# A residual taken from normalised tiles: VectorE's add of the spikes uses a ratio per token, and GpSimd normalises x once less

## What is computed

```python
x = x + layernorm(attn(layernorm(x)))      # attn: time mix and channel mix, each ended by spikes
x = x + layernorm(ffn(layernorm(x)))       # ffn: ternary weights, swiglu, two hidden layers with gelu

def attn(x):                               # x here is already normalised once
    x = x + lif(time_mix(layer_norm(x, ln1_s, ln1_b), ...))
    x = x + lif(channel_mix(layer_norm(x, ln2_s, ln2_b), ...))
    return x
```

## Time and profile before

| | us |
|---|---|
| median of 3 runs (lowest to highest) | 785.07 (781.07 to 785.68) |
| profiled execution | 779.8 |
| its span | 777.8 |
| mean granted TensorE clock, share of full speed | 0.952 |
| TensorE busy | 620.4 (80%) |
| VectorE busy | 640.6 (82%) |
| ScalarE busy | 522.6 (67%) |
| GpSimd busy | 478.2 (61%) |

### The profile page before, as it was taken

The page is one execution under the profiler, slowest core; times in us unless marked ns, Lnnn a source line. Parts: engine busy times, 40 slices in busy tenths (PEclk is TensorE's granted clock), DMA queues, the critical chain, the costliest instruction groups (busy, mean ns, idle before and its releaser), DMA issues. The chain is left out here.

```text
span 777.8 us, 10326 instructions
## 1 busy us (share of the span) xinstructions
PE 620.4 (80%) x2241; PEld 368.2 (47%) x2241; DVE 640.6 (82%) x1585; ACT 522.6 (67%) x791; POOL 478.2 (61%) x592
## 2 busy tenths in 40 slices
PE   3165399888888979898888979898888979888884
PEld 1022146464545546464555546463545546455553
DVE  5889688998989898989889898989889898965541
ACT  2543376868687776858586776868587777857563
POOL 4333526767685857747585857757575858563533
PEclk9577589999999999999999999999999999999998
DMA  5020000000000000000000000000000000000000
GB/s 206 0 68 0 29 1 1 28 15 28 14 29 15 27 13 0 27 13 27 13 27 13 27 13 0 27 13 27 13 27 13 13 16 13 15 2 0 15 14 13
DMA packets 26384, 16.69 MB, mean 21 GB/s; under 512 B 1136, under 2 KB 25712, under 8 KB 26096
## 3 DMA queue, kind: packets, MB, share of 16 engines
q1 hardware_dynamic: 26352, 16.34, 6.9%
HBM read 12.14 MB, written 4.19 MB: 21 GB/s over the span
## 5 line engine op out<-in xcount | busy, mean ns | idle before, releaser
L1511 PE MATMUL p_f<-ac_lo,w_hi 128*128 128x512 f32 x320 | 145.7, 455 | 16.9 <-DVE ac_lo L291 9.1
L723 ACT ACTIVATE hid<-p_f,scale 128x512 f32<-128x512 f32 x128 | 87.9, 687 | 89.3 <-PE p_f L1511 89.3
L407 POOL TENSOR_TENSOR var<-mv,eps_row 128x4 f32<-128x4 f32 x64 | 34.3, 536 | 177.1 <-DVE mv L959 177.1
L1511 PE MATMUL p_f<-ac_hi,w_hi 128*128 128x512 f32 x320 | 129.5, 405 | 0.0
L1511 PE MATMUL p_f<-b_lo,w_hi 128*128 128x512 f32 x256 | 109.0, 426 | 2.8 <-DVE b_lo L291 1.2
L1511 PE MATMUL p_f<-b_hi,w_hi 128*128 128x512 f32 x256 | 101.1, 395 | 0.0
L718 ACT ACTIVATE ac_hi<-hid 128x512 fp32r<-128x512 f32 x128 | 80.8, 632 | 22.3 <-DVE hid L1160 20.2
L291 DVE TENSOR_TENSOR ac_lo<-hid,ac_hi 128x512 fp32r<-128x512 f32 x80 | 78.0, 987 | 20.9 <-ACT ac_hi L718 20.1
L1511 PEld LDWEIGHTS p_f<-ac_lo,w_hi 128*128 128x128 f32 x320 | 62.5, 195 | 53.8 <-issue 17.9
L420 POOL TENSOR_TENSOR rstd<-var,minus_half 128x4 f32<-128x4 f32 x64 | 82.4, 1288 | 2.5
L291 POOL TENSOR_TENSOR ac_lo<-hid,ac_hi 128x512 fp32r<-128x512 f32 x48 | 66.6, 1400 | 17.3 <-ACT ac_hi L718 17.3
(11 more groups left out here) (129 smaller groups left out, 1501.1 us busy)
## 6 DMA issues: line engine op xcount, KB each, us to landing
xa<-in_x SPq DMA_DIRECT2D x16, 256.0 KB, 2.8
xb<-in_x SPq DMA_DIRECT2D x16, 256.0 KB, 3.1
out<-y_out SPq DMA_DIRECT2D x16, 256.0 KB, 2.3
kk<-in_ffn SPq DMA_DIRECT2D x1, 1024.0 KB, 6.0
hid<-in_ffn SPq DMA_DIRECT2D x1, 1024.0 KB, 8.6
hid<-in_ffn SPq DMA_DIRECT2D x1, 768.0 KB, 4.2
mix<-in_mix SPq DMA_DIRECT2D x1, 512.0 KB, 6.4
mix<-in_mix SPq DMA_DIRECT2D x1, 320.0 KB, 3.5
```

Of the source, the lines that this page charges most:

```text
L407: pool.tensor_tensor(var[n][:, :], mv[n][:, :, 1], eps_row[:, :], ALU.add).then_inc(s_var[n], 1)
L723: act.activation(hid[:, m], p_f[m % 2][:, :], ACT.Gelu, scale=scale[:, 1 + layer, m:m + 1]).then_inc(s_gelu[layer], 1)
L1511: last = pe.matmul(out_, w[:, b], x[:, k], start=(k == 0 and t == 0), stop=(k == n - 1 and t == len(terms) - 1))
```

## The change

x1 is no longer stored. Since n1 and x1 are the same centred tile times two factors per token, x1 = n1 x rstd1[0] / rstd1[1], and 1 / rstd1[1] = rstd1[1] x var1[1]. GpSimd makes this ratio as `back1` in two products of 128x4 (`back_1`, in the place of `norm_0`), and VectorE's `add_1` computes n1 x back1 + spikes, tile by tile. n1 gets a second buffer, so that it lives until `add_1`. The waits move with it: `norm_1` waits for TensorE's turn and for `add_1` of two groups before, `moments_1` for the variances instead of x1, and the load of xa for n1 alone. The negated mean of norm 1 goes.

```diff
--- before.py
+++ after.py
@@ -98,7 +98,7 @@
         half_row = sb("half_row", [P, T])
         minus_half = sb("minus_half", [P, 2, J])
         minus_one = sb("minus_one", [P, J])
-        neg_mean = {n: sb(f"neg_mean{n}", [P, J]) for n in (1, 3, 5)}
+        neg_mean = {n: sb(f"neg_mean{n}", [P, J]) for n in (3, 5)}
         eps_row = sb("eps_row", [P, J])
         ident = sb("ident", [P, P])
         ident16 = sb("ident16", [P, P], BF16)
@@ -106,12 +106,13 @@
 
 
         xa = sb("xa", [P, 2, J, C])
-        x1 = sb("x1", [P, 2, J, C])
-        n1 = sb("n1", [P, J, C])
+        n1 = sb("n1", [P, 2, J, C])
         bn1 = sb("bn1", [P, J, 6])
         mv1 = sb("mv1", [P, J, 2])
         var1 = sb("var1", [P, 2, J])
         rstd1 = sb("rstd1", [P, 2, J])
+        root1 = sb("root1", [P, J])
+        back1 = sb("back1", [P, 2, J])
         z1 = sb("z1", [P, NB, T + 1])
         d1 = sb("d1", [P, NB, T])
         mixed1 = sb("mixed1", [P, 3, NB, T])
@@ -204,7 +205,8 @@
         s_xb = [sem(f"s_xb{k}") for k in range(2)]
         s_bn = {n: sem(f"s_bn{n}") for n in (1, 2, 3, 4, 5)}
         s_mv = {n: sem(f"s_mv{n}") for n in (1, 2, 3, 4, 5)}
-        s_x1 = sem("s_x1")
+        s_root1 = sem("s_root1")
+        s_back1 = sem("s_back1")
         s_n = {n: sem(f"s_n{n}") for n in (1, 2, 3, 4, 5)}
         s_turned = {n: sem(f"s_turned{n}") for n in (1, 2, 4, 5)}
         s_z1 = sem("s_z1")
@@ -265,7 +267,7 @@
         s_y_out = sem("s_y_out")
         s_stored = sem("s_stored")
         s_var = {n: sem(f"s_var{n}") for n in (1, 2, 3, 4, 5)}
-        s_neg_mean = {n: sem(f"s_neg_mean{n}") for n in (1, 3, 5)}
+        s_neg_mean = {n: sem(f"s_neg_mean{n}") for n in (3, 5)}
         s_rstd = {n: sem(f"s_rstd{n}") for n in (1, 2, 3, 4, 5)}
 
         s_apart = sem("s_apart")
@@ -328,7 +330,6 @@
         def _(sp):
             def load_a(g):
 
-                wait(sp, s_x1, g.n - 1)
                 wait(sp, s_n[1], g.n - 1)
                 sp.dma_start(xa[:, g.par], x_tiles[g.n]).then_inc(s_xa[g.par], 16)
 
@@ -397,6 +398,7 @@
                 pool.wait_ge(s_mv[n], g.n + 1)
                 wait(pool, s_rstd[n], g.n)
                 if n == 1:
+                    wait(pool, s_back1, g.n)
 
 
                     apart(pool)
@@ -406,7 +408,7 @@
                 else:
                     pool.tensor_tensor(var[n][:, :], mv[n][:, :, 1], eps_row[:, :], ALU.add).then_inc(s_var[n], 1)
                 if n in neg_mean:
-                    pool.tensor_tensor(neg_mean[n][:, :], (mv1 if n == 1 else mv[n])[:, :, 0], minus_one[:, :],
+                    pool.tensor_tensor(neg_mean[n][:, :], mv[n][:, :, 0], minus_one[:, :],
                                        ALU.mult).then_inc(s_neg_mean[n], 1)
 
             def rstd(n, g):
@@ -474,9 +476,13 @@
                         pool.drain()
                 pool.engine_nop().then_inc(s_spikes[k], 1)
 
-            def norm_0(g):
+            def back_1(g):
+
+                pool.wait_ge(s_rstd[1], g.n + 1)
+                pool.tensor_tensor(root1[:, :], rstd1[:, 0], rstd1[:, 1], ALU.mult).then_inc(s_root1, 1)
                 wait(pool, s_x2, g.n - 1)
-                centered(1, g, x1[:, g.par], xa[:, g.par], rstd1[:, 0]).then_inc(s_x1, 1)
+                pool.wait_ge(s_root1, g.n + 1)
+                pool.tensor_tensor(back1[:, g.par], root1[:, :], var1[:, 1], ALU.mult).then_inc(s_back1, 1)
 
             def norm_3(g):
                 wait(pool, s_xres, g.n)
@@ -528,7 +534,7 @@
                 if on["wkv"]:
                     shift_2(g)
                 if on["shift_k"]:
-                    norm_0(nxt)
+                    back_1(nxt)
 
             def turn(pair, step, on):
                 nxt, g, c, f, done = (Group(pair, step + k) for k in (1, 0, -1, -2, -3))
@@ -965,7 +971,7 @@
 
             def moments_1(g):
                 wait(dve, s_n[1], g.n)
-                wait(dve, s_x1, g.n)
+                wait(dve, s_var[1], 2 * g.n)
                 moments(1, g, bn1, mv1)
 
             def centered(n, g, out_, in_, mv, rstd):
@@ -977,8 +983,9 @@
                 return last
 
             def norm_1(g):
-                wait(dve, s_turned[1], g.n)
-                centered(1, g, n1, xa[:, g.par], mv1, rstd1[:, 1]).then_inc(s_n[1], 1)
+                wait(dve, s_turned[1], g.n - 1)
+                wait(dve, s_x2, g.n - 1)
+                centered(1, g, n1[:, g.par], xa[:, g.par], mv1, rstd1[:, 1]).then_inc(s_n[1], 1)
 
             def norm_2(g):
                 wait(dve, s_turned[2], g.n)
@@ -1090,11 +1097,15 @@
 
             def add_1(g):
                 dve.wait_ge(s_spk_tok[0], g.n + 1)
-                dve.wait_ge(s_x1, g.n + 1)
+                dve.wait_ge(s_n[1], g.n + 1)
+                dve.wait_ge(s_back1, g.n + 1)
                 wait(dve, s_x3, g.n - 1)
                 wait(dve, s_n[2], g.n - 1)
-                dve.tensor_tensor(x2[:, g.par], p_spk[:, 0].rearrange("p (j c) -> p j c", c=C), x1[:, g.par],
-                                  ALU.add).then_inc(s_x2, 1)
+                spk = p_spk[:, 0].rearrange("p (j c) -> p j c", c=C)
+                for j in range(J):
+                    last = dve.scalar_tensor_tensor(x2[:, g.par, j], n1[:, g.par, j], back1[:, g.par, j:j + 1],
+                                                    spk[:, j], ALU.mult, ALU.add)
+                last.then_inc(s_x2, 1)
 
             def stats_2(g):
                 dve.wait_ge(s_x2, g.n + 1)
@@ -1394,7 +1405,7 @@
 
                     wait(pe, s_f0_lo, g.n - 2)
                     wait(pe, s_f_out, g.n - 3)
-                    turned(1, g, n1)
+                    turned(1, g, n1[:, g.par])
 
                 def turn_2(g):
                     pe.wait_ge(s_n[2], g.n + 1)
```

## The result

The changed kernel takes 820.21 us (median of 4 runs, 817.49 to 823.13) against 784.26 for the kernel before (also 4 runs now, 781.07 to 785.68): a ratio of 1.0448, with a 95% interval of 1.0419 to 1.0477. The forecast was slower, by 26 us; it is 36, and 820.21 lies above the upper end of the range, 817.

A forecast was written before the change was run, and what follows sets the result against it. VectorE's work plus its round-trip latencies was taken as the bound. Port collisions 13 x 1.6 = 20.8 and add_1 16 x 0.35 = 5.6 gave 26.4 us more: 806 or 811 by base, forecast 810, range 791 to 817.

The forecast's parts named there:

- What bounds the kernel: Whole turn of 43.10 us: VectorE's work (busy 38.98) plus the latencies of its round trips sets its length.
- GpSimd's part: GpSimd beside norm_4: norm_0 (2.89 us) out, two 128x4 products (0.6) in; 2.3 us free per turn, subtractions start earlier.
- The rival that made the kernel faster through rstd1: Turn start: rstd1 and first weighted sum 0.7 us earlier in 13 turns, 9.1 us, so 779 or 776; chance 0.08.
- The port term: At norm_4: GpSimd's two low(3) subtractions take the shared SBUF ports; VectorE loses 1.6 us in each of 13 turns.
- The last turn of before: Last full turn, without norm_0: norm_4 takes 2.94 us instead of 1.18, 1.76 lost; one tile read as held over both subtractions.
- The rival of a single collision: At norm_4 and bounds: only one subtraction collides, 13 x 0.5 + 5.6 = 12 us more, 797; chance 0.11.
- the one in which VectorE keeps the ports: VectorE holds the ports until ac_lo is done; only add_1 costs, 788 to 791; chance 0.14.
- The rule of the Trainium skill: Ports at norm_4: taken strictly, the two subtractions cost their whole 2.5 us, the sum about 10 us higher.
- The add: VectorE's add_1 as four operations: 1.04 us, 0.35 more per turn, counted in full in 16 turns, 5.6 us.
- The estimate set beside it: add_1 by the skill's 120 cycles plus length: 1.03 us against 0.66, 0.37 more; sum lower by under 1 us.
- the two terms: The sum: port collision at norm_4, 13 x 1.6 = 20.8 us, and add_1, 16 x 0.35 = 5.6 us.
- one of my two forecasts, 806: Whole program: 26.4 us added to the profiled execution's 779.8 gives 806; added to the runs' median, 785.07, gives 811.

The follow-up runs named there:

- both kernels with `y_out` moved: Kernel before, GpSimd's y_out addition put behind the first spikes' check: 765.49 us; the same with VectorE's f_out statistics ahead of norm_1: 763.06 us.
- the four adds: Kernel before with only add_1 changed, to four scalar_tensor_tensor of 128x128 with a column of ones; x1 still stored: 793.02 us, ratio 1.0104.
- GpSimd held: Changed kernel with GpSimd's low(3, 1) waiting until VectorE has done its last subtraction of layer 3: 789.81 us, ratio 1.0075.

## Why the prediction was wrong in size

**What bounds the kernel** was read rightly. VectorE's row with its round trips sets the turn: of 1.84 us lost in one place 1.77 was still there at `add_1`, 32 us later, and 0.85 saved in another place shortened the turn by 0.85.

**GpSimd's part** was right: the two products take 0.5 us with the gap between them, the subtractions start at once, and none of GpSimd's freed time shows in the turn. The rival that made the kernel faster through rstd1 had its deciding point right: the weighted sum follows the scans.

**The port term** was the right mechanism and a little too small: 1.84 us instead of 1.6, since the last tiles of `norm_4` were held by the full amount and VectorE's wait of 0.37 us for ScalarE absorbed nothing. That is 13 x 0.24 = 3 us. The last turn of before, one odd turn out of 16, gave the size to within 0.1. One reading of it was wrong: no tile was held over both subtractions. There the first tile (698.05, 1.21 us) was held by the first and the second (699.18, 1.30 us) by the second, the same pairs that the changed kernel shows for its third and fourth tile. The rival of a single collision and the one in which VectorE keeps the ports fell with the first row of the trace. The rule of the Trainium skill (SBUF — State Buffer, "SBUF: two separate sides") that the ports are locked for a whole instruction names the mechanism, and the trace agrees as far as each held tile ends just behind a subtraction. Charged at their whole length the two subtractions would have cost 2.58 us (in the prediction's figures 13 x 0.9 = 12 us more than its sum, not about 10); the rows show 1.84, as the second tile still ran to 365.90, 0.24 us into the first subtraction, and each held tile was done 0.09 us behind GpSimd instead of starting its 0.34 there.

**The add** was 1.12 us instead of 1.04, and 0.3 us of the turn instead of 0.35: the operations behind it met GpSimd's differently. The estimate set beside it, 0.37 us more, would have raised the sum by 16 x 0.02 = 0.3 us and not lowered it; measured on the operations themselves it is 1.12 - 0.69 = 0.43. I had charged the add in full by way of `xres` and `ac_lo`; in fact `ac_lo` escaped and `mixed` was held.

**The missing term was TensorE's clock.** This is the step that failed. I read the turn of 44.70 us in the earlier trace rows, took it for scatter that a kernel has or has not, and gave it no term in the sum and no place in the range: "The runs differ by how many turns fall at the lower clock, 1.5 us each" was right, but I let the number of such turns stand as it was. With the two terms as measured the sum is 13 x 1.84 + 16 x 0.3 = 29 us, which gives 813, inside the range. Most of the other 7 of the 36 us is the clock's. An estimate from the two kernels with the wait for the spikes filled: filling it takes 8.6 us off the changed kernel and 5.8 off the one before, so these drops cost 2.8 us more than they did. What is left between the two filled kernels is 32.5 us, 3.8 more than the two terms. Of that, the drops behind `norm_4`, which the kernel before does not have in these turns, make about 3.4: the 12 intervals of the filled changed kernel last 545.8 us instead of 12 x 45.2.

The two profiled executions differ by more, 39.0 us in their spans. The intervals of the turns 2 to 14 are 11.3 us beyond 12 x 45.2 in the changed kernel and 4.7 beyond 12 x 43.1 before, 6.6 more. The last interval between two `norm_4` is 2.8 longer, and that is not the change's doing. Here it is before, after, and in the kernel before with the wait for the spikes filled:

```profile
698.05:733.18 35.13, 29.54 (x117) 20.16 (x117) 19.35 (x48) 22.96 (x37) 16.96 (x23) 1.00 0.03 8
732.77:770.70 37.93, 32.09 (x117) 21.73 (x117) 19.41 (x49) 23.28 (x37) 16.85 (x23) 0.91 0.03 8
694.89:732.89 38.00, 32.37 (x117) 21.73 (x117) 19.37 (x48) 23.18 (x37) 16.88 (x23) 0.91 0.03 8
```

The third kernel still stores x1 and has the long interval at a clock of 0.91 all the same; so have both kernels with `y_out` moved and nothing else of the change or the filling in them, with 37.7 and 38.0 us. The profiled execution of the kernel before, 779.8 us, happened to be faster than every other run of it (781.07 to 788.89), and I had built one of my two forecasts, 806, on it.

**What stays open** is what decides in which turns the clock falls. The wait for the spikes is 1.12 to 1.19 us in the turns of all these kernels in which it was not filled. In the profiled executions the number of long intervals out of 12 is 3 for turns of 43.1 us, 7 for 43.4 with the four adds, 4 for 43.4 with GpSimd held, 3 for 44.9, 6 for 45.2, and none in the kernels with turns of 42.2 to 42.5 or below. That is no rule of length, and each number is that of one execution: the ten runs of the kernel with GpSimd held lie 10 us apart, and the one with 4 is the fastest of them. I have shown that filling the wait removes the drops, not what selects the turns.

## What to carry to other kernels

Before an operation is taken off an engine that is not the bound, look at what it stands in front of. Where GpSimd's next operation is a large one on SBUF and VectorE works from SBUF to SBUF beside it, the freed engine can take the ports from the busy one, as it did here at 1.84 us a turn. In this kernel an order in which GpSimd's large operations lie beside VectorE's PSUM reads and statistics was worth more than the operation saved. Look in the odd turns of the trace, the first and the last, for the overlap that the change will make: it may stand there with its price. And where TensorE has short waits on a path that VectorE waits for, count the turns at the lower clock as a term of the sum, with both ends in the range: in the profiled executions here, with this wait unchanged, their number went from none to 7 of 12.

## What the runs showed of the hardware

- A wait of TensorE of only 1.18 us, with one of 0.61 us shortly ahead of it, stood in front of a drop of the granted clock to 0.50 in some turns and not in others, and four products of 128x512 put into it removed the drops, in two kernels. What such a drop cost was not the same everywhere: about 1.65 us at the spikes, for which VectorE's `add_1` waits, and up to 0.6 us behind `norm_4`.
- GpSimd's four operations of 128x128 with one SBUF input hardly hold VectorE up: `norm_4` took 1.18 us beside them and 1.12 with GpSimd waiting; they themselves took 2.89 us. Its subtractions of 128x512 with two inputs do: 1.84 us for two of them.
- A scalar_tensor_tensor from SBUF is held as well: `mixed` took 1.80 us instead of 0.74 when it fell beside GpSimd's `xres` and `d`.
